# Padding the contraction of a bias product to 128 rows, and moving one relation's products and the fills of a queue

## The chip, the cores and the metric

One core of a Trainium2 chip runs the kernel. The metric is the device time of one execution in microseconds (us), median of the runs shown. Engine names as in the profile: PE is TensorE's matmul stream, PEld its weight loads, DVE VectorE, ACT ScalarE, POOL GpSimd, SP SyncE, which here only issues DMAs.

## The reference

A chain of graph layers over 625 nodes of width 512, with 10000 edges (`src`, `dst`, a type of three, a scalar weight):

```python
xr = einsum('nd,rde->rne', x, W_rel)              # three relations
msg = xr[edge_type, edge_src] + b_rel[edge_type]
h0 = relu(segment_sum(msg, edge_dst) + xs[node_type] + b_self[node_type])
# three mean layers (matmuls, layer norm), then four GINE layers:
e = edge_attr @ We + be;  m = relu(x[src] + e)
h = ((1 + eps) * x + segment_sum(m, dst)) @ W1 + b1
h = relu((h - mean_over_nodes) * rsqrt(var + 1e-5) * gamma + beta)
x = relu(h @ W2 + b2)
# one more mean layer with a sigmoid gate; residuals and norms between the layers
```

## The kernel before, in words

Nodes stand in five tiles of 125 rows (R = 125, NT = 5), the width in KT = 4 chunks of 128. A float32 product is made of two fp32r parts per operand, high and low, and three of the four part products (`THREE`): one output tile is 4 x 3 = 12 matmuls of 512 columns (`natural`, L710; the matmul is L715). ACT writes the high part of every operand, DVE the low part as a difference (`w_high`/`w_low` for weights, `tr_high`/`tr_low` for transposed activations). Weight matrix j goes into buffer W[j % 2]; a consumer waits for `w_split`. All queues run in the order in which they are written; semaphores join them.

**Relations stage.** `rel_tile(r, n)` (L763) makes tile n of relation r: 12 matmuls, then a thirteenth (L773) that adds the bias by contracting two rows: `one2` (two rows of ones) against `BREL` (high and low part of the bias row). ACT's `rel_copy` takes the result out of PSUM, SP stores it to DRAM. Beside this the edges are sorted into 83 tiles of 128: eight groups (NSG = 80 / 10 = 8) of one-hot matrices, `slot_onehots(g)` on DVE and `slot_weights(g)` on ACT, 10 activations or, for g = 1 and 5, 20 (not in `VEC_W`); PE contracts them in `slot_group(g)` (L775), 20 matmuls into bank 7. The buffers of a group are two, so group g+2 waits for group g's use. PE's order is: the five tiles of relation 0; then for g = 0..7 one further tile and `slot_group(g)`; then the last two tiles. DVE makes the low parts of relation 1's weights, `w_lows(1)`, only after the sorting chain (L1541 to L1558), which ends in `lohi`; those of relation 2, `w_lows(2)`, between groups 3 and 4, and `w_lows(3)` (first self weights) after group 7. ACT makes `w_highs(2)` after group 2's weights and `w_highs(3)` after group 7's. When group 7 is in, DVE makes the records (`rec_made`), PE finishes its tiles and counts edges (L849), and POOL gathers rows (L677) once the last tile is stored.

**GINE layers.** Each of the four layers l = 0..3 is a loop over the 83 edge tiles (gather L1041, scatter L1057), then the node part: five closes of PSUM (L725), `g_tile` on DVE (L2007), transposes on PE (L707), `tr_high` on ACT (L1109), `tr_low` on DVE, eight jobs of 12 matmuls for W1 (L1081, `HJOBS`), each followed by an ACT evacuation (L1414), a batch norm over nodes (`root_h`, `h_norm`, `h_high`, `h_low`), and 60 matmuls for W2 (L1096) behind five bias products (L751), which contract two rows of `BIAS` with the same `one2`. The 29 tiles that are gathered by POOL from DRAM land in a queue of 16 buffers Q; 23 of them are prefilled by ACT with weight times the `we` row (`queue_set`, L1321) before POOL adds the gathered row. For layers 0 to 2, ACT prefills entries of the next layer during the node part: k = 0..4 (`SET_T` = 5) straight after the loop, ahead of the three `tr_high`; k = 5, 6, 7 (to `SET_G` = 8) after `w_highs(13 + 2l)`, ahead of the first job's evacuation; k = 8 and 9 after jobs 3 and 5; k = 10..13 after `w_highs(14 + 2l)`. The first waits for the new `we` row (`web_load` on SP, issued when all fills and adds of the layer are done). Layer 3 has no such fills, as no further layer follows.

Of the kernel before, what the change touches and what calls it, by code (L numbers as in the profile page):

```python
# [16 lines left out]
P = 128  # L17
N = 625
D = 512
# [39 lines left out]
SET_T, SET_G, SET_W1, SET_W2 = 5, 8, 10, 14  # L59
# [35 lines left out]
DEG_AT = 4  # L95
W4_AT, W5_AT, W6_AT, W7_AT = 10, 24, 50, 72
# [16 lines left out]
def build(nc, x, src, dst, etype, ew, ntype, weights, b_rel, b_self, b1_l1, ln_g, ln_b,  # L113
# [8 lines left out]
    with ExitStack() as ctx:  # L122
# [124 lines left out]
        BREL = at(g_at, 14336, "b_rel_parts", [2, NREL, D], F32R)  # L247
# [40 lines left out]
        one2 = sb("one2", [2, ND], F32R)  # L288
# [186 lines left out]
        def _(sp):  # L475
# [52 lines left out]
            sp.dma_start(BREL[:, :, :].bitcast(F32), rw_d[:, B_REL:B_REL + NREL, :]).then_inc(small_in, 16)  # L528
# [175 lines left out]
        def _(pe):  # L704
# [45 lines left out]
            def bias(bank, k):  # L750
                return pe.matmul(ps[0:R, bank, :], one2[:, 0:R], BIAS[0:2, k % 2, :], start=True, stop=False)  # L751
# [37 lines left out]
            for n in range(NT):  # L789
                rel_tile(0, n)  # L790
            for g in range(NSG):
                rel_tile(1 + g // NT, g % NT)
# [7 lines left out]
            for n in range(NSG - NT, NT):  # L800
                rel_tile(2, n)
# [304 lines left out]
        def _(act):  # L1106
# [70 lines left out]
            for n in range(2, NT):  # L1177
                rel_copy(0, n)
            for g in range(NSG):
                slot_weights(g)  # L1180
                if g == 2:
                    w_highs(2)
                if g < NSG - 1:
                    rel_copy(1 + g // NT, g % NT)
            w_highs(3)
            for q in range(NSG - 1, 2 * NT):
# [179 lines left out]
            for l in range(NL2):  # L1366
# [25 lines left out]
                if l < NL2 - 1:  # L1392
                    for k in range(SET_T):
                        act.wait_ge(z_made, l * TE + STEP[TF + QR + k] + 1)
                        queue_set(l + 1, k)
# [3 lines left out]
                if l < NL2 - 1:  # L1399
                    for k in range(SET_T, SET_G):  # L1400
                        queue_set(l + 1, k)
# [10 lines left out]
                for i, (o, h) in enumerate(HJOBS):  # L1412
# [8 lines left out]
                    if l < NL2 - 1 and i in (3, 5):  # L1421
                        queue_set(l + 1, SET_G + (i - 3) // 2)
# [25 lines left out]
        def _(v):  # L1448
# [5 lines left out]
            v.memset(one2[:, :].bitcast(F32), 1.0).then_inc(dve_step, 1)  # L1454
# [68 lines left out]
            for a in range(2):  # L1523
# [16 lines left out]
                                 vd[:, :].unsqueeze(2).broadcast_to([P, NT, NT]), ALU.add))  # L1540
            v.tensor_tensor(ext[:, 0, :, :], run[:, :, :], oh[:, :, :], ALU.mult)  # L1541
# [56 lines left out]
            w_lows(1)  # L1598
# [18 lines left out]
            for g in range(1, 4):  # L1617
                slot_onehots(g)
            w_lows(2)
            for g in range(4, 6):  # L1620
# [495 lines left out]
```

## Time and profile before

| | us |
|---|---|
| median of 3 runs (865.6 to 866.92) | 865.64 |
| the profiled execution | 863.98 |
| its span | 862.2 |
| PE busy | 783.3 (91%) |
| DVE busy | 678.5 (79%) |
| ACT busy | 536.0 (62%) |
| granted TensorE clock, mean | 0.971 |

The span runs from the first to the last instruction of the profiled execution, and 1.8 us of its time lie around it. Busy shares are unions of intervals; matmuls are pipelined, so that the time between two starts is what a matmul costs PE, and a busy time of one is longer than that. A clock of 1.00 stands for 2.4 GHz, one of 0.5 for 1.2 GHz.

### The profile page before, as it was taken

To read this page: it belongs to the slowest core of one execution; us is meant where nothing else is said; L and a number is where in the kernel's file an instruction comes from. 1 tells how busy PE (TensorE), PEld (TensorE's weight loads), DVE (VectorE), ACT (ScalarE), POOL (GpSimd) and SP (SyncE) were. 2 spreads that over 40 slices of the span, in tenths; PEclk is the share of its full clock that TensorE was granted. 3 is DMA by queue.
4 is the path that set the end of the run, shared out by engine and by line. 5 is a ranking of instruction groups with operands and counts; after the bars stand their busy time and mean duration, and the time that the engine had idled before them with its cause. 6 is when DMAs were issued, how large, how long until landed. Compare 5 with 4: busy or idle time off the path is not lost.

```text
span 862.2 us, 12184 instructions
## 1 busy us (share of the span) xinstructions
PE 783.3 (91%) x3648; PEld 597.4 (69%) x3648; DVE 678.5 (79%) x1269; ACT 536.0 (62%) x1007; POOL 268.5 (31%) x230
## 2 busy tenths in 40 slices
PE   4799899899699799969999999989999999999895
PEld 3577565577377578757777777776777867778674
DVE  8995745899865978786897788977889878898635
ACT  3286115566562423556897678877788677875656
POOL 4000477774000000017750077400863018720000
PEclk9899999899799999988999999999999999999998
DMA  6223576786173130419993199723996249951101
GB/s 172 86 72 97 163 203 188 245 256 188 55 274 131 46 127 13 148 36 211 218 221 99 50 225 233 195 85 93 224 228 158 87 122 204 231 121 57 42 6 54
DMA packets 61330, 122.13 MB, mean 142 GB/s; under 512 B 9096, under 2 KB 22698, under 8 KB 61269
## 3 DMA queue, kind: packets, MB, share of 16 engines
q0 software_dynamic: 22096, 52.18, 27.7%
q1 hardware_dynamic: 39173, 69.17, 25.3%
q8 instruction: 34, 0.56, 0.3%
q14 instruction: 27, 0.22, 0.1%
HBM read 105.60 MB, written 15.73 MB: 141 GB/s over the span
## 4 chain that ended last, share of the span: by engine, by line
PE 62%; DVE 19%; ACT 9%; DMA 6%; issue 3%; SPq 1%; ACTq 0%; DVEq 0%
PE ps L715 13%; PE ps L1057 10%; PE ps L1041 7%; PE ps L1096 7%; PE ps L1081 6%; DVE z_parts L1998 5%; PE ps L830 4%; DMA onehot_dst<-onehot_rows 4%; PE ps L976 3%; PE ps L922 3%; DVE gathered_parts L1745 2%; ACT queued L1321 2%; DVE w L1480 2%; PE ps L860 2%; PE ps L707 2%
## 5 line engine op out<-in xcount | busy, mean ns | idle before, releaser
L683 POOL DMA_INDIRECT queued<-node_rows,srci x92 | 145.3, 1579 | 194.5 <-DMA node_rows<-work 152.1
L1057 PE MATMUL ps<-z_parts,onehot_dst 128*125 128x512 f32 x664 | 190.0, 398 | 4.0 <-DMA onehot_dst<-onehot_rows 2.8
L715 PE MATMUL ps<-w,xT 128*125 128x512 f32 x660 | 166.9, 405 | 6.8 <-DVE w L1480 5.8
L1998 DVE SCALAR_TENSOR_TENSOR z_parts<-ps,z_parts 128x512 fp32r<-128x512 f32 x216 | 146.3, 688 | 30.7 <-ACT z_parts L1381 25.3
L1381 ACT ACTIVATE z_parts<-ps 128x512 fp32r<-128x512 f32 x216 | 128.2, 596 | 49.6 <-PE ps L1041 41.5
L1057 PEld LDWEIGHTS ps<-z_parts,onehot_dst 128*125 128x125 f32 x664 | 120.4, 185 | 43.1 <-issue 15.3
L715 PEld LDWEIGHTS ps<-w,xT 128*125 128x125 f32 x660 | 122.6, 190 | 37.3 <-DVE w L1480 6.1
L1041 PE MATMUL ps<-x_parts,gather_lhs 128*128 x408 | 130.0, 401 | 0.5 <-DVE z_parts L1998 0.5
L1041 PEld LDWEIGHTS ps<-x_parts,gather_lhs 128*128 128x128 f32 x408 | 76.7, 189 | 20.4 <-issue 3.0
L1998 DVE SCALAR_TENSOR_TENSOR z_parts<-queued,z_parts 128x512 fp32r<-128x512 f32 x116 | 79.5, 685 | 6.1 <-ACT z_parts L1381 6.0
L677 POOL DMA_INDIRECT gathered<-rel_rows,rowi x75 | 75.7, 1010 | 23.6 <-issue 20.7
L1381 ACT ACTIVATE z_parts<-queued 128x512 fp32r<-128x512 f32 x116 | 73.2, 631 | 0.8 <-PE ps L1057 0.2
L1081 PE MATMUL ps<-x_parts,w 128*128 128x312 f32 (+1 forms) x384 | 59.8, 314 | 5.5 <-ACT x_parts L1109 5.5
L1321 ACT ACTIVATE queued<-we_rows,wt 128x512 f32<-128x512 f32 x92 | 62.1, 714 | 3.5 <-DMA we_rows<-in_we 2.7
L1208 ACT CAST gathered_parts<-gathered 128x512 fp32r<-128x512 f32 x75 | 45.0, 619 | 29.7 <-PE ps L922 29.4
L1081 PEld LDWEIGHTS ps<-x_parts,w 128*128 128x128 f32 x384 | 56.9, 193 | 7.4 <-issue 5.0
L696 POOL TENSOR_TENSOR work<-x_cur,be_rows 125x512 f32<-125x512 f32 x5 | 6.4, 1284 | 178.0 <-DVE work L1971 170.0
L1480 DVE TENSOR_TENSOR w<-w_stage,w 128x512 fp32r<-128x512 f32 x88 | 56.5, 686 | 6.5 <-ACT w L1113 6.5
L922 PE MATMUL ps<-gathered_parts,onehot_dst 128*125 128x512 f32 x166 | 53.5, 428 | 8.2 <-DVE gathered_parts L1745 8.2
L1113 ACT CAST w<-w_stage 128x512 fp32r<-128x512 f32 x88 | 49.6, 619 | 16.7 <-DMA w_stage<-in_weights 15.5
L1745 DVE TENSOR_TENSOR gathered_parts<-gathered,gathered_parts 128x512 fp32r<-128x512 f32 x75 | 49.4, 689 | 9.7 <-ACT gathered_parts L1208 9.7
L1096 PE MATMUL ps<-w,xT 128*125 128x512 f32 x240 | 57.1, 397 | 0.0
(295 smaller groups left out, 1112.9 us busy)
## 6 DMA issues: line engine op xcount, KB each, us to landing
w_stage<-in_weights SPq DMA_DIRECT2D x88, 256.0 KB, 3.7
onehot_dst<-onehot_rows SPq DMA_DIRECT2D x80, 250.0 KB, 5.2
onehot_rows<-onehot_dst SPq DMA_DIRECT2D x20, 250.0 KB, 2.3
gather_lhs<-edge_src_rows SPq DMA_DIRECT2D x8, 432.0 KB, 7.9
node_rows<-work SPq DMA_DIRECT2D x20, 160.0 KB, 2.0
queued<-node_rows,srci POOLq DMA_INDIRECT x116, 6.7
node_rows<-work SPq DMA_DIRECT2D x20, 90.0 KB, 2.0
rel_rows<-rel_rows_out SPq DMA_DIRECT2D x10, 160.0 KB, 1.9
```

The lines of the kernel that those rows point to most:

```text
L677: gp.indirect_dma_start(G[place(i)][:, :], None, xr_d, bass.IndirectOffsetOnAxis(ap=rowi[:, t:t + 1], axis=0)).then_inc(gath[arrival(i)], 16)
L683: gp.indirect_dma_start(Q[k % QR][:, :], None, xb_d, row, compute_op=ALU.add)\
L715: mm = pe.matmul(ps[0:R, bank, :], lt[:, a, k, n * R:(n + 1) * R], w[:, b, k, :], start=first and k == 0 and (a, b) == THREE[0], stop=last ...
L922: mm = pe.matmul(psf[0:R, bass.ds(d, D)], S[:, i // SK % SR, i % SK, :], M[:, i % MR, a, :], start=False, stop=False, skip_group_check=True)
L1041: mm = pe.matmul(ps[:, 5 + t % 3, :], L[:, t, :], XSF[:, bass.ds(s + a * NT * D, D)], start=a == HI, stop=a == LO)
L1057: mm = pe.matmul(psf[0:R, bass.ds(d, D)], S[:, j // SK % SR, j % SK, :], Z[:, g % ZR, a, :], start=False, stop=False, skip_group_check=True)
L1081: mm = pe.matmul(ps[:, HBANKS[i], 0:HC[h]], W[0][:, a, k, o * P:(o + 1) * P], GT[:, b, k, HC[0] * h:HC[0] * h + HC[h]], start=k == 0 and a ...
L1096: mm = pe.matmul(ps[0:R, n, :], XT[:, a, k, n * R:(n + 1) * R], W[1][:, b, k, :], start=False, stop=k == KT - 1 and (a, b) == THREE[-1])
L1321: nc.scalar.activation(Q[k % QR][:, :], WEB[:, :], ACT.Copy, scale=wt[:, TF + k:TF + k + 1])\
L1381: nc.scalar.activation(Z[:, g % ZR, HI, :], of, ACT.Relu).then_inc(z_hi, 1)
L1480: v.tensor_tensor(W[j % 2][:, LO, k, :], WS[:, k, :], W[j % 2][:, HI, k, :].bitcast(F32), ALU.subtract).then_inc(w_split, 1)
L1998: v.scalar_tensor_tensor(out=Z[:, g % ZR, LO, :], in0=of, scalar=0.0, in1=Z[:, g % ZR, HI, :].bitcast(F32), op0=ALU.max, op1=ALU.subtract) ...
```

## The change

1. `one2` and `BREL` have 128 rows instead of two. DVE fills both with zeros first, then rows 0 and 1 of `one2` with ones; the bias DMA writes rows 0 and 1 of `BREL`. The 15 products at L773 contract 128 rows. The 20 at L751 still contract two.
2. PE makes three tiles of relation 1 ahead of group 0, no tile ahead of group 0 otherwise, one ahead of each of groups 1 to 5, none ahead of 6 and 7, two after 7. ACT's copies follow that order.
3. `w_lows(1)` moves on DVE ahead of the products L1541 of the sorting chain; `w_lows(2)` ahead of group 3; `w_lows(3)` between groups 6 and 7. On ACT `w_highs(2)` moves from group 2 to group 1, and `w_highs(3)` to group 4.
4. In layers 0 to 2 none of the fills k = 0..9 stands ahead of `tr_high` or of job 0's evacuation: behind the evacuations of jobs 1 to 6 stand 2, 2, 1, 2, 1, 2 of them.

```diff
-SET_T, SET_G, SET_W1, SET_W2 = 5, 8, 10, 14
+SET_JOB = (0, 2, 4, 5, 7, 8, 10, 10)
+SET_W1, SET_W2 = SET_JOB[-1], 14
+REL_FIRST, REL_LAST = 3, 8
-        BREL = at(g_at, 14336, "b_rel_parts", [2, NREL, D], F32R)
+        BREL = at(g_at, 14336, "b_rel_parts", [P, NREL, D], F32R)
-        one2 = sb("one2", [2, ND], F32R)
+        one2 = sb("one2", [P, ND], F32R)
-            sp.dma_start(BREL[:, :, :].bitcast(F32), rw_d[:, B_REL:B_REL + NREL, :]).then_inc(small_in, 16)
+            sp.dma_start(BREL[0:2, :, :].bitcast(F32), rw_d[:, B_REL:B_REL + NREL, :]).then_inc(small_in, 16)
-                return pe.matmul(ps[0:R, bank, :], one2[:, 0:R], BIAS[0:2, k % 2, :], start=True, stop=False)
+                return pe.matmul(ps[0:R, bank, :], one2[0:2, 0:R], BIAS[0:2, k % 2, :], start=True, stop=False)
...
 # PE
             for n in range(NT):
                 rel_tile(0, n)
+            for i in range(REL_FIRST):
+                rel_tile(1, i)
             for g in range(NSG):
-                rel_tile(1 + g // NT, g % NT)
+                i = g + REL_FIRST - 1
+                if g and i < REL_LAST:
+                    rel_tile(1 + i // NT, i % NT)
                 slot_group(g)
...
-            for n in range(NSG - NT, NT):
-                rel_tile(2, n)
+            for i in range(REL_LAST, 2 * NT):
+                rel_tile(1 + i // NT, i % NT)
...
 # ACT
+            for q in range(REL_FIRST - 1):
+                rel_copy(1, q)
             for g in range(NSG):
                 slot_weights(g)
-                if g == 2:
+                if g == 1:
                     w_highs(2)
-                if g < NSG - 1:
-                    rel_copy(1 + g // NT, g % NT)
-            w_highs(3)
-            for q in range(NSG - 1, 2 * NT):
+                q = g + REL_FIRST - 1
+                if q < REL_LAST:
+                    rel_copy(1 + q // NT, q % NT)
+                if g == 4:
+                    w_highs(3)
+            for q in range(REL_LAST, 2 * NT):
                 rel_copy(1 + q // NT, q % NT)
...
-                if l < NL2 - 1:
-                    for k in range(SET_T):
-                        act.wait_ge(z_made, l * TE + STEP[TF + QR + k] + 1)
-                        queue_set(l + 1, k)
                 for n in range(3):
                     tr_high(GBANK[n], GT, n, TR_L2[l] + n + 1)
                 w_highs(13 + 2 * l)
-                if l < NL2 - 1:
-                    for k in range(SET_T, SET_G):
-                        queue_set(l + 1, k)
...
-                    if l < NL2 - 1 and i in (3, 5):
-                        queue_set(l + 1, SET_G + (i - 3) // 2)
+                    if l < NL2 - 1 and i:
+                        for k in range(SET_JOB[i - 1], SET_JOB[i]):
+                            if QR + k < TL:
+                                act.wait_ge(z_made, l * TE + STEP[TF + QR + k] + 1)
+                            queue_set(l + 1, k)
...
 # DVE
-            v.memset(one2[:, :].bitcast(F32), 1.0).then_inc(dve_step, 1)
+            link(v.memset(one2[:, :].bitcast(F32), 0.0))
+            v.memset(one2[0:2, :].bitcast(F32), 1.0).then_inc(dve_step, 1)
+            v.memset(BREL[:, :, :].bitcast(F32), 0.0).then_inc(dve_step, 1)
...
                                  vd[:, :].unsqueeze(2).broadcast_to([P, NT, NT]), ALU.add))
+            w_lows(1)
             v.tensor_tensor(ext[:, 0, :, :], run[:, :, :], oh[:, :, :], ALU.mult)
...
-            w_lows(1)
             slot_onehots(0)
...
-            for g in range(1, 4):
+            for g in range(1, 3):
                 slot_onehots(g)
             w_lows(2)
-            for g in range(4, 6):
+            for g in range(3, 6):
                 slot_onehots(g)
...
             for g in range(6, NSG):
                 slot_onehots(g)
-
-            w_lows(3)
+                if g == 6:
+                    w_lows(3)
+
```

## Rows read from the trace of the kernel before

**Rows 1.** Timeline of TensorE, relations stage: start us, us, engine, line, what [idle before].
```profile
40.10 5.12 PE L715 MATMUL ps<-w,xT 128*125 128x512 f32 x12 [5.81 <-DVE w L1480]
46.12 0.39 PE L721 MATMUL ps<-zero 128*128 128x512 bf16 x1 [0.48 <-DVE slot_values L1587]
...
53.34 3.05 PE L715 MATMUL ps<-w,xT 128*125 128x512 f32 x12
56.75 0.25 PE L781 MATMUL ps<-slot_values,slot_low 125*128 125x166 f16 x1
...
88.80 3.05 PE L715 MATMUL ps<-w,xT 128*125 128x512 f32 x12
91.78 0.49 PE L773 MATMUL ps<-b_rel_parts,one 2*125 2x512 f32 x1
92.20 0.70 PE L805 MATMUL ps<-ident,type_columns 125*3 125x125 f32 x5
```

**Rows 2.** The chain that ended last: start us, us, what, with its count.
```profile
27.70 2.24 DVE picked L1541
...
315.12 2.79 PE ps L715 x12
317.91 2.32 PE ps L976 x10
...
477.88 1.35 PE ps L751 x5
```

**Rows 3.** Windows of core 0: stretch, its us, busy us (count) by engine, granted clock, DMA share, GB/s.
```profile
34.00:41.00 7.00, 1.19 (x3) 0.81 (x3) 6.55 (x18) 0.58 (x1) 0.00 (x0) 0.77 0.12 37
46.10:85.40 39.30, 38.95 (x256) 30.00 (x257) 29.63 (x68) 31.38 (x106) 0.00 (x0) 1.00 0.25 76
```

**Rows 4.** Timeline of VectorE and ScalarE, relations stage, columns as in rows 1.
```profile
39.35 2.50 DVE L1480 TENSOR_TENSOR w<-w_stage,w 128x512 fp32r<-128x512 f32 x4
...
51.11 0.81 DVE L1578 TENSOR_TENSOR slot_low<-iota_pairs,lohi 125x1280 bf16<-125x1280 f16 x1
54.59 0.82 DVE L1578 TENSOR_TENSOR slot_low<-iota_pairs,lohi 125x1280 bf16<-125x1280 f16 x1
...
46.15 5.24 ACT L1170 ACTIVATE slot_weights<-slot_high,weight_parts 125x83 bf16<-125x83 bf16 x20
54.66 2.17 ACT L1113 CAST w<-w_stage 128x512 fp32r<-128x512 f32 x4
```

**Rows 5.** Timeline of all engines, node part of layer 1, columns as in rows 1.
```profile
560.91 3.17 ACT L1321 ACTIVATE queued<-we_rows,wt 128x512 f32<-128x512 f32 x5 [1.47 <-DMA we_rows<-in_we]
561.21 0.28 PE L725 MATMUL ps<-zero 128*128 128x16 bf16 x5
570.82 10.95 PE L1081 MATMUL ps<-x_parts,w 128*128 128x314 f32 x72 [0.64 <-ACT x_parts L1109]
581.70 1.42 PE L751 MATMUL ps<-bias_parts,one 2*125 2x512 f32 x5
```

**Rows 6.** The same of layer 3, which has no fills.
```profile
770.33 0.28 PE L725 MATMUL ps<-zero 128*128 128x16 bf16 x5
776.77 12.47 PE L1081 MATMUL ps<-x_parts,w 128*128 128x312 f32 x84
789.16 1.42 PE L751 MATMUL ps<-bias_parts,one 2*125 2x512 f32 x5
793.55 0.73 ACT L1410 ACTIVATE xT<-work 128x626 fp32r<-128x626 f32 x1 [1.97 <-DVE work L2031]
```

**Rows 7.** The same of layers 0 and 2, first and last step.
```profile
457.46 0.28 PE L725 MATMUL ps<-zero 128*128 128x16 bf16 x5
477.81 1.42 PE L751 MATMUL ps<-bias_parts,one 2*125 2x512 f32 x5
...
666.48 0.29 PE L725 MATMUL ps<-zero 128*128 128x16 bf16 x5
686.64 1.42 PE L751 MATMUL ps<-bias_parts,one 2*125 2x512 f32 x5
```

## The prediction

> **What bounds the kernel now.** I read four views: the chain that ended last, for the places where PE is not what decides; the timeline of each such place; windows for the clock; and the node part of one layer beside another that lacks the moved work. Two places matter.
>
> In the relations stage PE has no work from 34.3 to 40.10: the idle before the first tile of relation 1 is 5.81 us and ends with DVE's low weight parts [rows 1]. Those are made behind the sorting chain, at 39.35 [rows 4]. From 46.12 on PE is the bound: in 46.10 to 85.40 it is busy 38.95 of 39.30, DVE and ACT only 29.6 and 31.4 [rows 3]. Group 7 ends at the end of that window, the last tile at 92.20.
>
> In the node part of layers 0 to 2 ACT is the bound. In layer 1 the fills start at 560.91, after 1.47 us of waiting for the `we` row, and last 3.17; PE's closes stand at 561.21, so the transposed activations wait behind the fills [rows 5]. Later PE waits 0.64 for the last `tr_high`, behind fills 5 to 7 [rows 5]. Layer 3 is this node part without fills.
>
> **The change part by part.**
>
> *The bias product.* From a tile's first matmul to the next work is 92.20 - 88.80 = 3.40 us behind a tile, and 56.75 - 53.34 = 3.41 behind a group [rows 1]. 12 full products follow each other in 2.79 (0.233 each), and the ten behind them, which contract 125 rows, in 2.32 (0.232) with no gap between [rows 2]. So 13 equal slots are 3.03, and the two-row product costs 0.38 more than a slot. It isn't its own length: five of them in a row take 1.35, 0.27 each with their edges [rows 2]. The excess lies at the edges: 2.98 from first matmul to bias for twelve slots of 0.233 = 2.79, and 0.42 from the bias to the next [rows 1]. With 128 rows I take 3.05 per tile (a slot, and a little for the change of type behind a group): 0.35 less on each of 15. Bounds: 0.38, and nothing. Of relation 0's five, 1.7 us fall into the idle time ahead of relation 1; the ten others are on PE's path, 3.5 us at most.
>
> The Trainium skill speaks on both sides. Its page "TensorEngine Tiling (Array Packing)", section "Key Properties", says that a change of tiling mode drains the engine, which the two edges agree with. Its page "TensorE: Matmul & The Clock Gate", section "LDWEIGHTS (loading the stationary operand)", says that the rows contracted don't change the time, only the columns do. By that alone the padding would bring nothing; this is a rival below.
>
> *The zero fills.* Two more memsets of DVE stand in its first 4 us, where it waits for the edges; by size 1.5 us, and that idle time is about 1.9. Nothing, or 0.3 if it overruns.
>
> *Order in the relations stage.* `w_lows(1)`, 2.5 us [rows 4], now runs from 27.7 on, where L1541 began [rows 2]. DVE's total up to `slot_onehots(0)` stays, so group 0 is ready at 46.1 as before [rows 1]. PE makes three tiles by 33 + 3 x 3.05 = 42, then waits about 4 us for group 0 instead of 5.81 and 0.48. From there I went forward with fixed costs, each step starting at the latest of its engine and of what it waits for. Costs: tile 3.05, group 1.8 (46.12 to 53.34 holds the zeros, two groups and a tile of 3.40), DVE per group 3.48 (51.11 to 54.59) or a product of 0.5 less where ACT has the twenty, four low parts 2.5, ACT 2.6 per ten activations (5.24 for twenty), four high parts 2.1, a copy 0.5 [rows 1, 4]. Group 0 ends at 48.0, group 1 at 52.9, group 2 at 57.7, group 3 at 62.6, group 4 at 67.4: PE without a gap, but a cycle is 4.85 instead of 5.2. Then ACT becomes the bound: its copy of relation 2's second tile waits for PE (65.6), `w_highs(3)` adds 2.1, group 5's twenty 5.1, to 73.3. PE waits 2.7 for it. DVE's one-hot for group 7 waits for the same (the buffer rule), then `w_lows(3)` stands in front of group 7, which is ready at 81.3. So group 7 ends at 83.2, the last two tiles at 89.3. The same steps in the old order give 84.9 and 91.7 (measured 85.4 and 92.2, so the method is 0.5 short in both). Group 7 comes 1.7 earlier, the tiles 2.4.
>
> Behind that the counting starts with the later of PE's tiles and DVE's records and first one-hots. The records follow group 7 by 3.7, the one-hots by 6.3, so 89.5, against zeros on PE that only follow at 89.3 + 2: the tiles decide, 2.4. SP's stores of the last tile and with them POOL's gathers follow the tiles too, so both shift. `w_load(2)` and `w_load(3)` on SP stand behind stores that come earlier now.
>
> From 2.4 I take off 0.9 for the clock. Before, the idle 5.81 brought TensorE to 1.2 GHz: the window 34 to 41 has a clock of 0.77, and the twelve matmuls behind it took 5.12 instead of 3.05 [rows 1, 3]. That fell in front of a wait for group 0 and cost nothing. Now the 4 us wait may do the same ahead of group 0, and from there to group 4 PE has no gap to hide it; the waits of 2.7, 1.2 and 3.1 between groups 4 and 7 may do it again ahead of the last tiles. Each such fall costs up to 2 (5.12 - 3.05). I take 1.5 for the stage, with ends at -1.6 (slower) and +2.9.
>
> *The fills in the node part.* From the closes to the first bias product layer 3 takes 789.16 - 770.33 = 18.83, layer 1 581.70 - 561.21 = 20.49 [rows 5, 6], layers 0 and 2 20.35 and 20.16 [rows 7]. If the new layers 0 to 2 take 18.83: 1.52 + 1.66 + 1.33 = 4.5. The fills are still there, ten of 0.63 (3.17 for five [rows 5]) between evacuations. PE does not wait for those in its 84 matmuls in 12.47 [rows 6]; a job lasts 1.76. Two fills (1.27), an evacuation (0.45), and a root or `h_high` (0.3 or 0.65) are 2.0 to 2.4, one fill 1.4 to 1.7, so ACT falls behind by some 1.7 by job 7. What is late next: `h_high` of the last chunk, 4.39 behind the first bias product in layer 3 (793.55 - 789.16 [rows 6]), would be at 5.4, its low part done at 6.8. PE wants that chunk after five biases (1.36 [rows 2]), thirty matmuls for the first two chunks (7.0) and three more: 9.1 behind. 2.3 us are left. `w_highs(14 + 2l)` and fills 10 to 13 then end at 10.6 behind the bias; the first W2 tile is done at 9.8 to 10.1, so the first evacuation is 0.5 late, and ACT makes it up, with 1.2 of work per tile against 1.4 on PE. So 4.5, with bounds 2 (ACT late in every layer by 0.8) and 5.
>
> **The sum.** 863.98 - 1.5 - 4.5 = 858.0 for an execution like the profiled one. That one lies 1.66 under the median of the runs shown, so 859.6.
>
> **The rivals.**
> A. *The padding doesn't shorten the product* (the rule about rows). With 3.40 per tile the same steps give 93.3 for the last tile, 1.6 later than the old order gives, since three more waits come between groups and PE has lost none of its work. 863.98 + 1.6 - 4.5 + 1.66 = 862.7. The two 0.23 slots in [rows 2] and the gap at both edges speak against it.
> B. *The fills come back later.* ACT reaches the last chunk or the `x_parts` evacuations late, or the next loop's start is held by transfers anyway. 2 of 4.5 are left: 862.1. For it: ACT is busier than in layer 3 by 6.3 us in the same 19. Against it: 2.3 us of slack as above.
> C. *The clock takes nothing*, and one of its low stretches further down goes too: 4.5 + 2.9 + 1 = 8.4 less, 857.2.
> D. *Slower: the clock.* The place is the wait ahead of group 0 and those between groups 4 and 7. If each of three gives a low stretch as long as two of the one before, and such a stretch reaches dense work throughout, each microsecond at 1.2 GHz costs half of one. 6 us of gain are used up by 12 us more at 1.2 GHz on PE's path. With 20 us it would be 859.6 + 10 - 0.9 = 868.7. Against it: in 46.10 to 85.40 a clock of 1.00 with PE waits of 0.3, and the new groups still bring 1.8 us of matmuls after each wait.
>
> **How the numbers follow.** Forecast 0.62 (its own range 858 to 861.3), A 0.07, B 0.13, C 0.11, D 0.07. The runs shown spread by 1.3 us, so 0.2%, 1.7 us, is about what can be told from no change. All but D lie below 863.9; the upper end of B and A and the mildest of D lie within 0.2%. Faster 0.88, same 0.06, slower 0.06. The range reaches over A, B and C: 856.6 to 863.2.
>
> **What would show it.** Bias to next matmul 0.23 and 3.03 to 3.05 per tile at L773, and still 0.27 at L751. No wait for L1480 at 40; a wait of 4 us ahead of L721 at 46. The counting (L849) at 92 to 93 instead of 94.47. From L725 to L751 about 18.8 in layers 0 to 2, no L1321 ahead of L1109, and no PE wait ahead of the 84 matmuls. The forecast is wrong if a tile stays at 3.40, if the W2 matmuls (L1096) of layers 0 to 2 wait for ACT, or if the clock's mean falls under 0.96.

## The result, and the profile after

| us | before | after |
|---|---|---|
| median | 866.14 (5 runs) | 859.34 (857.95 to 862.34, 5 runs) |
| ratio of runs, 95% interval | | 0.9914 (0.9885 to 0.9943) |
| the profiled execution, its span | 863.98, 862.2 | 859.34, 857.6 |
| PE busy | 783.3 | 781.7 |
| granted clock, mean | 0.971 | 0.973 |

The forecast was 859.6 in 856.6 to 863.2. The total came out, and one of its two terms did not: the node parts gave what the prediction said (4.5 us), the relations stage gave nothing (forecast 1.5).

PE's timeline of the kernel after, relations stage, from the end of relation 0's tiles on (start us, us, engine, line, operation, what it waited for; L717 is the matmul of a tile, L775 its bias product, L723 the zeros ahead of group 0, L783 the first matmul of a group):

```profile
30.05 2.96 PE L717 MATMUL ps<-w,xT 128*125 128x512 f32 x12
32.85 0.39 PE L775 MATMUL ps<-b_rel_parts,one 128*125 128x512 f32 x1
...
41.96 0.39 PE L775 MATMUL ps<-b_rel_parts,one 128*125 128x512 f32 x1
45.91 0.39 PE L723 MATMUL ps<-zero 128*128 128x512 bf16 x1 [3.56 <-DVE slot_values L1596]
48.86 3.68 PE L717 MATMUL ps<-w,xT 128*125 128x512 f32 x12
...
54.42 3.05 PE L717 MATMUL ps<-w,xT 128*125 128x512 f32 x12
...
75.56 0.24 PE L783 MATMUL ps<-slot_values,slot_low 125*128 125x166 f16 x1 [2.73 <-ACT slot_weights L1176]
78.60 0.23 PE L783 MATMUL ps<-slot_values,slot_low 125*128 125x166 f16 x1 [0.99 <-ACT slot_weights L1176]
83.49 0.25 PE L783 MATMUL ps<-slot_values,slot_low 125*128 125x166 f16 x1 [2.86 <-DVE slot_values L1596]
86.27 3.73 PE L717 MATMUL ps<-w,xT 128*125 128x512 f32 x12
89.83 0.40 PE L775 MATMUL ps<-b_rel_parts,one 128*125 128x512 f32 x1
90.06 2.94 PE L717 MATMUL ps<-w,xT 128*125 128x512 f32 x12
...
93.07 0.70 PE L811 MATMUL ps<-ident,type_columns 125*3 125x125 f32 x5
```

Beside [rows 1]: a full-clock tile takes 3.01 (90.06 to 93.07) where it took 3.40, and from bias to next work it is 0.23 where it was 0.42. PE no longer waits at 34 to 40, but 3.56 us ahead of group 0. The last tile ends at 93.07, not at 92.20. The counting of edges, which the prediction had at 92 to 93, begins at 95.43 (94.47 before).

Where the granted clock was at half, beside the wait ahead of it (windows: stretch, its us, busy us and count by engine, granted clock, DMA share, GB/s):

```profile
42.35:45.90 3.55, 0.00 (x0) 0.00 (x0) 3.40 (x7) 3.55 (x14) 0.00 (x0) 1.00 0.01 2
46.84:50.25 3.41, 3.41 (x18) 2.79 (x16) 3.12 (x12) 3.41 (x15) 0.00 (x0) 0.50 0.07 26
80.63:83.48 2.85, 0.00 (x0) 0.00 (x0) 2.80 (x6) 0.37 (x2) 0.00 (x0) 1.00 0.00 0
84.39:87.80 3.41, 3.41 (x18) 2.76 (x16) 1.25 (x8) 0.00 (x0) 0.00 (x0) 0.50 0.00 0
```

PE is idle in the first and third stretch, and about 1 us into the dense work that follows, the clock falls to 1.2 GHz. In [rows 3] the low clock stood in PE's idle time and in front of a wait, and 46.10 to 85.40 was at 1.00; now both low stretches hold nothing but work.

The node part of layer 1, all engines (L1087 is W1's matmul, L1115 `tr_high`, L1331 a fill, L1413 `h_high`, L753 W2's bias product):

```profile
557.71 0.28 PE L727 MATMUL ps<-zero 128*128 128x16 bf16 x5
...
559.53 1.90 ACT L1115 CAST x_parts<-ps 128x500 fp32r<-128x500 f32 x3 [3.58 <-PE ps L709]
...
564.15 12.47 PE L1087 MATMUL ps<-x_parts,w 128*128 128x312 f32 x84
...
566.58 1.32 ACT L1331 ACTIVATE queued<-we_rows,wt 128x512 f32<-128x512 f32 x2
...
576.54 1.42 PE L753 MATMUL ps<-bias_parts,one 2*125 2x512 f32 x5
...
581.53 0.73 ACT L1413 ACTIVATE xT<-work 128x626 fp32r<-128x626 f32 x1 [1.97 <-DVE work L2040]
```

The closes to the first bias product take 18.83 in place of 20.49 [rows 5]: no fill ahead of `tr_high`, which now waits for PE instead, and PE's 84 matmuls in the 12.47 of layer 3 [rows 6].

Where the time went in the two profiled executions, after against before, at the same step: counting starts +0.96; first gather of layer 0 -1.92; behind layer 0's node part -4.71; layer 1's -5.15; layer 2's -7.33; end of layer 3's W2 -7.62; end -4.64. The three node parts are -1.53, -1.66 and -1.34, together -4.53. What else moved lies between steps that the change doesn't touch, and has two sources. One is where the low stretches of the clock fall: the kernel after has 48.2 us of them in all, the one before 51.6, but not in the same places. One in the aggregation was 3.41 us long in place of 6.83, and two behind layer 3's W2 were new:

```profile
801.18:804.59 3.41, 3.41 (x10) 2.52 (x9) 2.21 (x6) 1.94 (x4) 0.00 (x0) 0.50 0.00 0
821.66:825.07 3.41, 3.41 (x9) 2.63 (x9) 0.00 (x0) 0.11 (x1) 0.00 (x0) 0.50 0.00 0
```

These two took back 3 us between two steps that no edit touches. All fourteen traces of this study agree on the price: from the end of layer 3's W2 to the end it is 57.45 to 57.48 us where no low stretch falls in between but the one in which every trace ends (four traces, the kernel before among them), 58.94 to 59.04 with one more of 3.41 (nine), and 60.44 with these two. So one such stretch on dense work costs 1.5 us. The other source is not the clock: from layer 0's W2 to layer 1's closes it took 69.00, before 67.78, with no low stretch in either. Over all traces and the three loops in question this step varies from 66.94 to 69.37, with none in any of them.

This is why single executions of one kernel differ by several us, and why below a place in the trace decides on an edit, and a ratio on the kernel. A place varies too. The relations stage is the same in the kernel before and in e1 below, and its counting starts at 94.47 and 95.01; it is the same in the changed kernel and in e4, with 95.43 and 96.68. A difference of about 1.2 us in the start of the counting shows nothing by itself.

### The profile page after: what moved, and what is told of

It reads as the page before. It is cut to its first block, busy times and chain, and to the rows that moved or that the text cites. A ratio compares the mean times of both kernels' runs of the same rounds, so it can differ in the third digit from the quotient of the medians.

```text
span 857.6 us, 12186 instructions
## 1 busy us (share of the span) xinstructions
PE 781.7 (91%) x3648; PEld 599.1 (70%) x3648; DVE 679.9 (79%) x1271; ACT 536.0 (62%) x1007; POOL 272.4 (32%) x230
## 4 chain that ended last, share of the span: by engine, by line
PE 72%; DVE 15%; ACT 6%; DMA 4%; issue 2%; SPq 0%; POOL 0%; ACTq 0%; DVEq 0%; POOLq 0%
PE ps L1063 17%; PE ps L717 13%; PE ps L1047 10%; PE ps L1102 7%; PE ps L1087 7%; PE ps L836 4%; PE ps L982 3%; PE ps L928 3%; PE ps L709 2%; DVE gathered_parts L1754 2%; DVE w L1488 2%; PE ps L866 2%; DMA onehot_dst<-onehot_rows 2%; DVE st L1796 1%; DMA queued<-node_rows,srci 1%
## 5 line engine op out<-in xcount | busy, mean ns | idle before, releaser
L685 POOL DMA_INDIRECT queued<-node_rows,srci x92 | 148.1, 1610 | 185.3 <-DMA node_rows<-work 147.6
L717 PE MATMUL ps<-w,xT 128*125 128x512 f32 x660 | 169.6, 410 | 1.0 <-DVE xT L1483 1.0
L717 PEld LDWEIGHTS ps<-w,xT 128*125 128x125 f32 x660 | 125.8, 194 | 31.5 <-issue 1.2
L1331 ACT ACTIVATE queued<-we_rows,wt 128x512 f32<-128x512 f32 x92 | 62.6, 714 | 0.0
L1087 PE MATMUL ps<-x_parts,w 128*128 128x312 f32 (+1 forms) x384 | 57.7, 309 | 3.0 <-ACT x_parts L1115 3.0
L1119 ACT CAST w<-w_stage 128x512 fp32r<-128x512 f32 x88 | 49.6, 618 | 16.0 <-DMA w_stage<-in_weights 14.7
L1087 PEld LDWEIGHTS ps<-x_parts,w 128*128 128x128 f32 x384 | 55.6, 189 | 4.1 <-issue 3.9
L1488 DVE TENSOR_TENSOR w<-w_stage,w 128x512 fp32r<-128x512 f32 x88 | 56.5, 686 | 2.2 <-ACT w L1119 2.2
L1102 PE MATMUL ps<-w,xT 128*125 128x512 f32 x240 | 57.1, 397 | 0.0
```

The costliest lines, as they stand in the source:

```text
L685: gp.indirect_dma_start(Q[k % QR][:, :], None, xb_d, row, compute_op=ALU.add)\
L717: mm = pe.matmul(ps[0:R, bank, :], lt[:, a, k, n * R:(n + 1) * R], w[:, b, k, :], start=first and k == 0 and (a, b) == THREE[0], stop=last ...
L1087: mm = pe.matmul(ps[:, HBANKS[i], 0:HC[h]], W[0][:, a, k, o * P:(o + 1) * P], GT[:, b, k, HC[0] * h:HC[0] * h + HC[h]], start=k == 0 and a ...
L1102: mm = pe.matmul(ps[0:R, n, :], XT[:, a, k, n * R:(n + 1) * R], W[1][:, b, k, :], start=False, stop=k == KT - 1 and (a, b) == THREE[-1])
L1488: v.tensor_tensor(W[j % 2][:, LO, k, :], WS[:, k, :], W[j % 2][:, HI, k, :].bitcast(F32), ALU.subtract).then_inc(w_split, 1)
```

## The experiments

My theory after the result: the padding's 0.39 a tile is real; the new order leaves its waits ahead of work that has no wait behind it, so that the clock falls on PE's path, and the high and low parts of the third weights (`w_highs(3)`, `w_lows(3)`) stand in front of groups 5 and 7; only the fills reach the end. The rival: the padding is worth something at the end too, and the order as well, and the difference of one execution is chance.

### One part at a time

**e1_fills.** The kernel before with part 4 alone:

```diff
+SET_JOB = (0, 2, 4, 5, 7, 8, 10, 10)
...
-                if l < NL2 - 1:
-                    for k in range(SET_T):
...
-                    if l < NL2 - 1 and i in (3, 5):
-                        queue_set(l + 1, SET_G + (i - 3) // 2)
+                    if l < NL2 - 1 and i:
+                        for k in range(SET_JOB[i - 1], SET_JOB[i]):
```

> The kernel before with part 4 alone: the fills k = 0..9 of the queue stand behind jobs 1 to 6 in layers 0 to 2. Theory (ACT's fills were what PE waited for in the node part): closes (L725) to first bias product (L751) 18.8 us in layers 0 to 2 in place of 20.35, 20.49 and 20.16, the relations stage unchanged with the counting at 94.5 us, time 4.5 us less, ratio about 0.995. Rival (the fills come back later): the step from closes to bias is shorter, but the W2 products or the next loop's start wait for it, time at most 2 us less, ratio 0.998 or more. Rival (clock): the layers gain 4.5, and stretches at 1.2 GHz come or go elsewhere by 1.7 us each, so a single execution lies between 2.8 and 6.2 less.

Measured: 861.68 (10 runs) against 865.14, ratio 0.9944 (0.9919 to 0.9969). Closes to bias 18.81, 20.31 and 18.84. The one of layer 1 has its first twelve W1 matmuls at half clock, which is no fill's doing (PE's timeline):

```profile
560.69 0.28 PE L726 MATMUL ps<-zero 128*128 128x16 bf16 x5
...
564.56 3.36 PE L1082 MATMUL ps<-x_parts,w 128*128 128x312 f32 x12 [0.76 <-ACT x_parts L1110]
568.67 12.40 PE L1082 MATMUL ps<-x_parts,w 128*128 128x312 f32 x84
```

3.36 in place of 1.96. So the theory came in two layers of three, and in the ratio. The fills alone give most of the gain, perhaps all of it: 4.8 us by the ratio, and its interval overlaps that of the whole change.

**e2_pad.** The kernel before with part 1 alone:

```diff
-        BREL = at(g_at, 14336, "b_rel_parts", [2, NREL, D], F32R)
+        BREL = at(g_at, 14336, "b_rel_parts", [P, NREL, D], F32R)
...
-        one2 = sb("one2", [2, ND], F32R)
+        one2 = sb("one2", [P, ND], F32R)
...
```

> The kernel before with part 1 alone: one2 and BREL with 128 rows, no order changed. Theory (two-row products cost their edges, 0.38 us a tile): at L773 bias to next 0.23 us, 3.03 to 3.05 a tile, the last group about 2.3 and the last tile about 3.0 us earlier than before, time 2.3 to 3 us less, ratio 0.997. Rival (rows don't matter to the time of a product): 3.40 a tile as before, ratio 1.000.

Measured: 865.82 (12 runs), ratio 1.0000 (0.9970 to 1.0029). In its trace the counting starts at 92.58, 1.90 earlier. A full-clock tile takes 3.03 (87.19 to 90.22), as the theory had it; the ratio is the rival's. The window that holds the wait ahead of relation 1, and PE's timeline there:

```profile
34.77:45.01 10.24, 4.96 (x12) 3.86 (x13) 9.53 (x24) 2.61 (x10) 0.00 (x0) 0.50 0.33 102
```
```profile
32.04 0.39 PE L773 MATMUL ps<-b_rel_parts,one 128*125 128x512 f32 x1
40.05 5.30 PE L715 MATMUL ps<-w,xT 128*125 128x512 f32 x12 [7.62 <-DVE w L1482]
```

PE comes to the wait earlier, waits 7.62 where it waited 5.81, and the low clock lasts 10.24 us. The first 1.7 us saved (five tiles of relation 0) become waiting, as the prediction had it; the next 1.9 reach the counting (the last tile ends 2.0 earlier, where 3.0 were expected); and the median of the runs shows none of it.

**e3_order.** The kernel before with parts 2 and 3, the bias products over two rows:

```diff
+REL_FIRST, REL_LAST = 3, 8
+            for i in range(REL_FIRST):
+                rel_tile(1, i)
...
-            w_highs(3)
+                if g == 4:
+                    w_highs(3)
```

> The kernel before with parts 2 and 3 alone: the order in the relations stage, with two-row products. Theory (the new order gives PE three tiles in its idle time, and gives it back in waits of 3 to 4 us ahead of groups 5 to 7, behind w_highs(3) on ACT and w_lows(3) on DVE, and in products at 1.2 GHz): counting 1.5 to 3 us later than before, at 96 to 97.5, ratio 1.002 to 1.003. Rival (the early tiles are a gain of their own): counting at 92.5 or earlier, ratio 0.998.

Measured: 866.20 (12 runs), ratio 1.0004 (0.9979 to 1.0030). The counting starts at 94.47, to the hundredth as before. PE waits 2.12, 2.45 and 2.44 ahead of groups 0, 5 and 7, and the last tiles start at 85.40, as in the old order. Neither expectation came: not the 1.5 to 3 us later of the theory, whose waits were to be 3 to 4, and not the 2 earlier of the rival. By the ratio the order alone is worth nothing either way, within 0.3%.

**e4_relations.** Parts 1 to 3 without the fills, so the changed kernel less part 4.

> The kernel before with parts 1, 2 and 3: the whole change of the relations stage, the fills as before. Theory of the trace of the changed kernel (counting at 95.43 in place of 94.47, the stage gained nothing): counting at 95 to 95.5 us, time 0.5 to 1 more than before apart from the clock elsewhere, ratio 0.998 to 1.002. Rival (the prediction's 1.5 us gain): counting at 93, ratio 0.998. The sum of this and the fills alone should be the changed kernel's 0.991 if the parts add, with the rest in the clock.

Measured: 864.87 (12 runs), ratio 1.0000 (0.9975 to 1.0025). The counting starts at 96.68, 2.21 later than before. PE waits 4.70 ahead of group 0, the clock is at half for 6.8 us from 44.92 and for 3.4 from 85.88. The ratio is the theory's: padding and order together gain nothing. The counting is 1.2 later than it said, by the longer low stretch at group 0.

Over all executions of these kernels (some 180, each with its mean clock) a common slope fits: 5.6 us less time for each 0.01 more of mean clock. At equal clock the kernels stand against the one before at -3.9 (after), -3.3 (e1), -2.2 (e2), +0.7 (e3), +0.2 (e4), each within about 1.1 (after 1.5). So e2's saving of some 2.2 us is there, and its mean clock, 0.963 against 0.968, takes it back. This is a description of the runs and not a cause: by the 1.5 us of a stretch of 3.41, 0.01 of mean clock would be some 7.6 us if every stretch fell on dense work (an estimate), so the slope of 5.6 mixes stretches that cost something with stretches in waits that cost nothing. That the padding lowers the clock by its longer wait is shown for the one stretch above, not for the mean.

### Holding the clock, and taking the parts out of the way

**e5_warm.** The changed kernel with matmuls of zeros in the wait ahead of group 0:

```diff
             for i in range(REL_FIRST):
                 rel_tile(1, i)
+            for i in range(14):
+                pe.matmul(ps[:, 7, :], zero[:, :], zero[:, :].unsqueeze(1).broadcast_to([P, D // P, P]),
+                          start=True, stop=True)
```

> The changed kernel with 14 products of zeros into PSUM bank 7 behind the third early tile, where PE waits 3.55 us for group 0 (14 x 0.216 = 3.0 us). They add nothing to the result. Theory (the wait brings TensorE to 1.2 GHz over group 0 and the tile behind it, 1.6 us on PE's path): the clock stays 1.00 from 42 to 53, group 0 takes 2.0 and the tile 3.05, and the counting starts 1.5 us earlier than in the changed kernel, at 93.9; ratio 0.990. Rival (zeros don't hold the clock, or the low stretch comes later all the same): counting at 95.4 as before, ratio 0.991 to 0.992.

Measured: 857.84 (12 runs) against 864.83, ratio 0.9932 (0.9906 to 0.9959); counting 94.36. PE's timeline:

```profile
41.85 3.19 PE L796 MATMUL ps<-zero 128*128 128x512 bf16 x14
46.38 0.39 PE L723 MATMUL ps<-zero 128*128 128x512 bf16 x1 [1.33 <-DVE slot_values L1599]
48.40 3.04 PE L717 MATMUL ps<-w,xT 128*125 128x512 f32 x12
...
82.38 0.25 PE L783 MATMUL ps<-slot_values,slot_low 125*128 125x166 f16 x1 [2.85 <-DVE slot_values L1599]
...
85.08 3.82 PE L717 MATMUL ps<-w,xT 128*125 128x512 f32 x12
```

Group 0 is ready no sooner, but the tile behind it takes 3.04 and not 3.68, and group 7 begins 1.1 earlier, for 1.5 forecast. That is no more than a place varies by, but the two steps themselves are shorter. The second low stretch, from 83.38, is still there. By the ratio it isn't told from the changed kernel, and the forecast 0.990 lies outside its interval. So the zeros are shown to hold the clock in this stretch, and not to make the kernel faster.

**e6_w3_late.** The changed kernel with the third weights' parts behind group 7, as in the kernel before:

```diff
 # ACT
-                if g == 4:
-                    w_highs(3)
+            w_highs(3)
 # DVE
-                if g == 6:
-                    w_lows(3)
+            w_lows(3)
```

> The changed kernel with w_highs(3) and w_lows(3) behind group 7, where they were in the kernel before. Theory (the stage lost its gain since group 5's weights wait behind w_highs(3) on ACT and group 7's one-hots behind w_lows(3) on DVE; the same steps as in the prediction with this order give group 7 4.4 us earlier): waits ahead of groups 5, 6, 7 of 0.7, 1.2 and 0.8 in place of 2.7, 1.2 and 2.85, last tile 4.4 us earlier, counting at 90 to 91.5, time 4 to 5 us less than the changed kernel, ratio 0.986 to 0.987. Rival (PE's wait ahead of group 5 comes from the copies that wait for PE, the waits stay): counting at 94 or later, ratio 0.990 or more.

Measured: 853.81 (6 runs), ratio 0.9883 (0.9849 to 0.9917); counting 90.38, 5.05 earlier than in the changed kernel. The theory came. First the changed kernel, ACT and then DVE (L1119 the high parts, L1488 the low parts, L1176 the weights of group 5):

```profile
68.11 2.18 ACT L1119 CAST w<-w_stage 128x512 fp32r<-128x512 f32 x4
70.19 5.23 ACT L1176 ACTIVATE slot_weights<-slot_high,weight_parts 125x83 bf16<-125x83 bf16 x20
78.20 2.49 DVE L1488 TENSOR_TENSOR w<-w_stage,w 128x512 fp32r<-128x512 f32 x4
```

PE's timeline of e6:

```profile
74.39 0.24 PE L783 MATMUL ps<-slot_values,slot_low 125*128 125x166 f16 x1 [0.66 <-ACT slot_weights L1176]
77.42 0.23 PE L783 MATMUL ps<-slot_values,slot_low 125*128 125x166 f16 x1 [0.99 <-ACT slot_weights L1176]
79.97 0.24 PE L783 MATMUL ps<-slot_values,slot_low 125*128 125x166 f16 x1 [0.51 <-DVE slot_values L1595]
...
81.88 3.05 PE L717 MATMUL ps<-w,xT 128*125 128x512 f32 x12
```

The wait ahead of group 5 falls from 2.73 to 0.66 (ACT's four high parts are 2.18), the one ahead of group 7 from 2.86 to 0.51 (DVE's four low parts are 2.49), and with the long wait the low clock behind it goes: group 7 takes 1.91 to the next tile and that tile 3.12 (81.88 to 85.00), not 2.78 and 3.79. Waits of 2.1 and 2.3 and clock of 1.5, less 0.9 by which the tile behind group 1 starts later here (55.33 against 54.42; the low stretch at group 0 was 6.8 us long), are 5.0. Five microseconds are four times what a place varies by.

**e7_late_warm.** Both of these edits.

> Both edits of the two runs beside it: products of zeros in the wait for group 0, and w_highs(3), w_lows(3) behind group 7. Theory (the two losses are separate): counting at 88.5 to 89.5, time 6 us under the changed kernel, ratio 0.984 to 0.985, the version that beats both. Rival (one of the two is no loss): the ratio of the better of the two alone.

Measured: 853.23 (6 runs), ratio 0.9873 (0.9837 to 0.9909); counting 88.30. One window shows why, with a clock of 1.00 and PE busy 43.91 of 49.00:

```profile
43.00:92.00 49.00, 43.91 (x296) 33.69 (x294) 41.05 (x97) 34.83 (x120) 1.70 (x2) 1.00 0.26 79
```

The counting came as early as expected, the time did not quite (0.984 to 0.985 forecast): of 6.17 us at the counting's start 4.64 are left at its end, since the one low stretch (from 92.67) now falls into it. This is the fastest kernel of the study. It beats the one before, and very likely the changed one: its highest run, 855.56, and that of e6, 857.65, lie below the lowest of that one, 857.95, though the intervals, of separate sets, overlap (0.9885 to 0.9909 for e7). How much of it the zeros bring beyond e6 is not told by the ratios (0.9873 and 0.9883).

**e11_all_between.** e7 with the two tiles kept for after group 7 put between the groups too:

```diff
-REL_FIRST, REL_LAST = 3, 8
+REL_FIRST, REL_LAST = 3, 10
```

> The changed kernel with the third relation's high and low parts behind group 7 and 14 matmuls of zeros behind the third early tile (the fastest so far, ratio 0.9873, counting 88.30), and the last two tiles that were kept for after group 7 put between the groups too (REL_LAST 10: tiles 3 to 9 of the order between groups, then the groups end). There TensorE waits 0.66, 0.98 and 0.51 us ahead of groups 5, 6 and 7 with no tile ahead of groups 6 and 7. Theory (these waits are for ScalarE's weights of the slots, and tiles put there fill them but their copies on ScalarE delay the weights in turn): the counting starts within 0.7 us of 88.30, ratio 0.986 to 0.988. Rival (the tiles fill the waits for nothing): counting 86.5, ratio 0.985.

Measured: 857.44 (6 runs), ratio 0.9900 (0.9868 to 0.9932); counting 92.57. Both expectations missed. PE's timeline:

```profile
83.94 0.17 PE L727 MATMUL ps<-zero 128*128 128x16 bf16 x1
83.96 0.69 PE L814 MATMUL ps<-ident,type_columns 125*3 125x125 f32 x5
89.38 0.41 PE L818 MATMUL ps<-ident,slf 128*54 128x128 f32 x1 [4.72 <-DVE wt L1670]
...
89.80 2.91 PE L723 MATMUL ps<-zero 128*128 128x512 bf16 x7
```

The tiles are done at 81.81 + 0.23, but group 7 ends 4.2 later than in e7, and behind it PE waits 4.72 for the records that DVE makes from group 7, and the clock falls there too (the seven zeros take 2.91, in e7 1.69). The two last tiles were the cover of that wait.

### Is it the clock alone?

**e9_before_warm** and **e10_pad_warm.** The kernel before, and e2, with 24 and 32 matmuls of zeros in the wait ahead of relation 1. In the one (in the other with 32):

```diff
             for n in range(NT):
                 rel_tile(0, n)
+            for i in range(24):
+                pe.matmul(ps[:, 7, :], zero[:, :], zero[:, :].unsqueeze(1).broadcast_to([P, D // P, P]),
+                          start=True, stop=True)
```

> The kernel before, with 24 matmuls of zeros (128x512, some 0.216 us each, 5.2 us in all) between the last early tile of relation 0 and the first of relation 1, where TensorE is idle for 5.80 us [before: 34.29 to 40.10] and the granted clock is at half from 37.83 for 6.83 us. They compute nothing that is used. Theory (the clock is the price of a wait): the half-clock stretch at 37.8 is gone, some 2.3 us of the tiles' work that it held (40.10 to 44.66) get back half their length, the counting starts near 92.2 in place of 94.47, and the time is about 863.5 (ratio 0.997). Rival (the clock is lowered somewhere in this stretch whatever is done): it comes back at 45 to 60, ratio 1.000.

> The kernel before with part 1 alone (the bias products of the relations over 128 rows padded with zeros) and 32 matmuls of zeros (6.9 us) where TensorE is idle for 7.62 us ahead of relation 1. To be read beside the kernel before with its idle filled in the same way: the two differ by the padding alone, with the clock held in both. Theory (padding saves 0.38 us a tile, and is given back as clock when the idle time ahead of relation 1 grows): now it shows, nine to ten tiles behind the wait at 0.38 us, 1.9 us at the counting as without the held clock and up to 3.5 where no wait takes it; counting near 89.5 to 90.5, time about 861 (ratio 0.994 to 0.995). Rival (the padding itself takes clock, since the array is busier): ratio as with the idle filled alone, 0.997, and half-clock stretches elsewhere.

Measured: e9 864.94 (12 runs), ratio 0.9988 (0.9966 to 1.0010), counting 95.72, 1.24 later than before; e10 864.38 (12 runs), ratio 0.9975 (0.9954 to 0.9996), counting 94.13. What I had called the theory missed twice (92.2, and 89.5 to 90.5), and the rivals came: in e9 the low stretch at 38 is gone, and another lies at 46.3. In e10 the ratio is the 0.997 of its rival, and the mean clock of its runs is below that of e9. PE's timeline of e9, and its window there:

```profile
33.03 5.35 PE L792 MATMUL ps<-zero 128*128 128x512 bf16 x24
39.78 3.09 PE L715 MATMUL ps<-w,xT 128*125 128x512 f32 x12 [1.40 <-DVE w L1483]
42.80 0.49 PE L773 MATMUL ps<-b_rel_parts,one 2*125 2x512 f32 x1
45.80 0.39 PE L721 MATMUL ps<-zero 128*128 128x512 bf16 x1 [2.51 <-DVE slot_values L1590]
```
```profile
46.34:49.75 3.41, 3.41 (x21) 2.83 (x19) 3.05 (x15) 3.41 (x15) 0.00 (x0) 0.50 0.19 57
```

At full clock the first tile of relation 1 is done at 43.29, 2.3 us sooner than in [rows 1] (46.12 less the wait of 0.48), and PE waits that much longer for group 0, which DVE still sets at 45.8. Behind this wait of 2.51 the clock falls on dense work, where before it had fallen ahead of a wait. So holding the clock is worth something only up to the last wait before the dense work: e5's zeros stand there, e9's one wait too early. e10 starts its counting 1.59 ahead of e9, with one low stretch of 3.41 from 46.3 in both; by the ratios the two aren't told apart. What the padding alone is worth at the end stays open below some 2.6 us (e2's interval).

The rival of e10, that the padding itself takes clock, isn't refuted. In both pairs with the old order the mean clock of the runs is 0.005 lower with the padding: 0.963 for e2 against 0.968 before, and 0.970 for e10 against 0.975 for e9, where the first wait is filled in both. In the new order it is not: 0.967 for e4 and for e3. At equal clock, as above, e9 stands at +3.0 and e10 at 0.0: the zeros raised e9's mean clock and brought no time, and between the two the padding is worth some 3 us, most of which its lower clock takes back. What lowers it stays open.

### What the edges of the bias product belong to

**e8_rows64**, **e12_rows96.** The changed kernel with L775 over the first 64, and over the first 96, of the padded rows:

```diff
-                pe.matmul(ps[0:R, bank, :], one2[:, 0:R], BREL[:, r, :], start=False, stop=True).then_inc(y_done, 1)
+                pe.matmul(ps[0:R, bank, :], one2[0:64, 0:R], BREL[0:64, r, :], start=False, stop=True).then_inc(y_done, 1)
```

> The changed kernel with the bias product contracting 64 of the padded rows. Theory (the cost lies in going between products that use up to half of the rows and products that use all): the edges come back, 0.32 before and 0.42 behind the product, 3.40 a tile. Rival (the cost grows with the rows left out): less than 0.38 of excess, as 0.2.

> The changed kernel with the relations' bias products over the first 96 of the 128 padded rows. With 64 rows the gaps at the edges are 0.326 into the product and 0.426 out of it, as with two; with 128 rows 0.233 on both sides. If the edges belong to any product whose rows are fewer than the array's, 96 rows show the same 0.33 and 0.43; if they belong to products that fit half the array (64 rows or fewer), 96 rows show 0.233 on both sides and 3.01 us a tile.

PE's timeline of e8, then of e12, last tile:

```profile
90.04 3.06 PE L717 MATMUL ps<-w,xT 128*125 128x512 f32 x12
93.03 0.50 PE L775 MATMUL ps<-b_rel_parts,one 64*125 64x512 f32 x1
93.45 0.70 PE L811 MATMUL ps<-ident,type_columns 125*3 125x125 f32 x5
```
```profile
90.20 2.95 PE L717 MATMUL ps<-w,xT 128*125 128x512 f32 x12
92.99 0.40 PE L775 MATMUL ps<-b_rel_parts,one 96*125 96x512 f32 x1
93.23 0.70 PE L811 MATMUL ps<-ident,type_columns 125*3 125x125 f32 x5
```

64 rows: 2.99 and 0.42, as with two. 96 rows: 2.79 and 0.24, as with 128. So the theory of e8 came, and the second of the two readings of e12. (One run each, 858.55 and 862.82, which say nothing of so small a difference.) The Trainium skill, "TensorEngine Tiling (Array Packing)", section "Available Configurations", lists row tilings of 128, 64 and 32 rows and none between; that a product of 64 rows has the edges and one of 96 has not agrees with it.

e8 shows a second thing. It is the changed kernel with the edges back, 0.39 on each of 15 tiles, and its counting starts at 95.72, against 95.43, 95.59 (e12) and 96.68 (e4) without them. PE waits 1.21, 2.44 and 2.19 ahead of groups 0, 5 and 7 in place of 3.56, 2.73 and 2.86. Seven tiles behind the first wait would be 2.7 us. In the new order what the padding saves goes into waits that DVE and ACT set, and into the clock behind them: e8 has no low stretch at group 0.

## Why the prediction was right or wrong

**The tile: right.** 3.05 for 3.40 was forecast; it is 3.01, the upper bound of 0.38 and a little more. Rival A (nothing) is out. The section of the Trainium skill that it leaned on ("TensorE: Matmul & The Clock Gate", "LDWEIGHTS (loading the stationary operand)") speaks of the load of the weights alone, and not of the whole product. A's price for the new order with tiles of 3.40 was wrong as well: 1.6 later, where e3 is 0.00 later. That 1.7 us of relation 0 turn into waiting was right too.

**The zero fills: right in the end.** DVE's second memset of zeros is 1.34 us, and the first work on the edges begins at 4.65 in place of 4.16, 0.5 later where at most 0.3 was forecast. But DVE still waits 0.50 for the edges ahead of it, and in e1, without these fills, it begins at 5.13, so the half microsecond isn't theirs. The zeros of group 0 stand at 45.91, before at 46.12.

**The waits of the new order: right, and read wrongly.** Forecast ahead of groups 5, 6, 7 were 2.7, 1.2 and 3.1; measured are 2.73, 0.99 and 2.86. The step named their causes, `w_highs(3)` and `w_lows(3)`, and then took them as given. e6 shows that they were the largest thing in the stage: without them the counting starts 5.05 us sooner. e3 has waits of 2.45 and 2.44 at the same places, and its counting starts as before, to 0.00; that they are what ate the gain of the early tiles there is likely, and was not run.

**The clock in the relations stage: the step that failed.** The prediction said that the wait of 4 us ahead of group 0 "may do the same", and the later ones "again ahead of the last tiles", each fall costing up to 2, and took off 0.9 for all. The mechanism was right and its size was not: two falls came on dense work. Group 0 and the tile behind it took 2.95 and 3.75 (45.91, 48.86, 52.61) where e5 at full clock took 2.02 and 3.11, and group 7 and the next tile 2.78 and 3.79 where e6 took 1.91 and 3.12: 1.6 and 1.5, so 3.1 for 0.9. The rest of the miss, some 0.3, is a cycle of 4.94 for 4.85 (54.42 to 59.36), and three small transposes behind group 4 that the steps left out. So the term -1.5 was +0.96 in this execution, +2.21 in e4's, and 0 by the ratio of e4. The bound on that side, 1.6 slower, held the first and the ratio, and not e4's trace.

**The fills: right.** 18.83 was forecast for layers 0 to 2; measured are 18.82, 18.83 and 18.83, and the sum is 4.5. `h_high` of the last chunk is 4.99 behind the bias (5.4 forecast), and no W2 matmul waits. What was saved doesn't come back in the loops either: the three that follow take 205.10 us in all, before 205.01. Rival B is out.

**The sum.** In the profiled pair -1.5 - 4.5 = -6.0 was forecast and -4.6 came: +1.0 in the relations stage, -4.5 in the node parts, and -1.1 in steps that the change doesn't touch, partly by low stretches that fell elsewhere and partly by loops that vary without them. That the median, 859.34, is so near to 859.6 is partly luck: the median of before was 865.64 in the runs shown and 866.14 beside the kernel after. Rival D named the right mechanism. Its 20 us are three stretches as long as the old one (6.83), though its sentence has them twice as long; there were two half as long. Rival C, that the clock takes nothing, is out by the same two.

## What to carry to other kernels

Work pulled ahead on an engine that feeds the critical one is paid by every wait it makes, so go through the order once with it and once without before taking it as given. Price a wait by where the clock would be low: in front of another wait it costs nothing, in front of dense work 1.5 to 1.6 us here for each stretch of 3.41. A few matmuls of zeros in the last wait before the dense work held it in three traces (e5, e7, e11), though no ratio here shows what that is worth. Before closing a gap behind the last step of a chain by moving work forward, see whether that work covers the next step's wait (e11), and whether a saved microsecond arrives at a wait that some other engine sets (e2, e8, e9). Before reading an edit from the start of a step in one trace, see how far that start moves between kernels that share everything up to it.

## What the runs showed of the hardware

- The extra time of an fp32r product over few rows lies at its edges. 2 rows and 64 rows alike take 2.98 to 2.99 us from the first matmul of the tile to the bias and 0.42 behind it; 96 and 128 rows take 2.79 and 0.23. Nearly 0.4 us each time that products of the two kinds alternate.
- Filling one wait with zeros removed a low stretch of the clock at 38 us and gave another at 46, behind the next wait (2.51 us), on dense work. What decides whether a wait brings a fall was not settled, and its length alone doesn't: the wait ahead of group 5 is 2.73 in the changed kernel and in e4, and 2.72 in e12, and only e12 has a low stretch behind it (from 77.10); in e3 one of 2.45 brought one, where a later wait hid it, and ones of 2.12 and 2.44 did not. The stretch from 821.66 in the changed kernel has a wait of only 0.63 close ahead of it. Kernels with the same relations stage had 3.41 us at half clock at group 0 (changed kernel) and 6.83 (e4, e12).
- A stretch of 3.41 us at half clock on dense work costs 1.5 us: the step behind layer 3's W2 is 57.45 to 57.48 us with none, 58.94 to 59.04 with one, 60.44 with two.
- Matmuls of zeros keep TensorE at 2.4 GHz: with 24 of them (5.35 us) e9 has no low stretch from 33 to 46.3, with 14 (3.19 us) e5 has none from 41.85 to 83.38.
